# The head and the four preparation stages of a four-layer attention and mixture-of-experts kernel: load order, shared norms, prepared probabilities, a split subtraction

## The reference, cut to what matters

```python
def _prob(x):
    x = jnp.tanh(x) * 0.499 + 0.5
    return jnp.clip(x / (jnp.sum(x, axis=-1, keepdims=True) + EPS), EPS)
q_prob = _prob(q)                 # q = _layernorm(x)
k_prob = _prob(k)                 # k = v = ctx
log_ratio = jnp.log(q_prob) - jnp.log(k_prob)
sid = jnp.einsum('bnd,bmd->bnm', q_prob - k_prob, log_ratio)
attn = jax.nn.softmax(-sid / D ** 0.5, axis=-1)
attn_feat = jnp.einsum('bnm,bmd->bnd', attn, v)
f_diff = (v - attn_feat) @ W_diff.T + b_diff + q
h = _layernorm(f_diff, ln_g, ln_b)
out = gelu(h @ W1.T + b1) @ W2.T + b2 + f_diff     # then a layernorm
```

## Time and profile before

| what | us |
|---|---|
| median of 3 runs (lowest, highest) | 1151.25 (1150.07, 1156.2) |
| span of the profiled execution | 1143.9 |
| TensorE busy | 982.2 (86%) |
| VectorE busy | 742.5 (65%) |
| ScalarE busy | 478.9 (42%) |
| GpSimd busy | 280.5 (25%) |

### The profile page before, as it was taken

The page is one execution under the profiler, slowest core; times in us unless marked ns, Lnnn a source line. Parts: engine busy times, 40 slices in busy tenths (PEclk is TensorE's granted clock), DMA queues, the critical chain, the costliest instruction groups (busy, mean ns, idle before and its releaser), DMA issues.

```text
span 1143.9 us, 20648 instructions
## 1 busy us (share of the span) xinstructions
PE 982.2 (86%) x6905; PEld 591.4 (52%) x6905; DVE 742.5 (65%) x1952; ACT 478.9 (42%) x1055; POOL 280.5 (25%) x242
## 2 busy tenths in 40 slices
PE   7878789878898799999998876898899898987893
PEld 3555455546465488888885442333333333335662
DVE  3484677684878766666663476578777857545665
ACT  3443725342433344444442320446666657532331
POOL 0333524523320233444331001100010011112551
PEclk8999989998998899999999997669999988677997
DMA  8442020003535411111115486233163041231225
GB/s 289 150 129 110 2 74 1 19 1 93 142 98 166 146 49 53 49 53 48 48 40 164 96 152 126 54 42 53 43 112 75 2 131 61 87 126 37 79 76 176
DMA packets 69506, 98.64 MB, mean 86 GB/s; under 512 B 6528, under 2 KB 56960, under 8 KB 66976
## 3 DMA queue, kind: packets, MB, share of 16 engines
q1 hardware_dynamic: 60000, 63.75, 20.3%
q0 software_dynamic: 9408, 33.56, 11.0%
HBM read 70.10 MB, written 27.13 MB: 85 GB/s over the span
## 4 chain that ended last, share of the span: by engine, by line
PE 50%; DVE 28%; ACT 7%; DMA 7%; issue 4%; POOL 2%; SPq 1%; DVEq 0%; ACTq 0%; POOLq 0%
PE pb L1004 11%; PE pb L1021 7%; DVE MX L1943 5%; PE pb L1109 4%; PE pb L1022 3%; PE pb L769 3%; PE pb L1133 2%; PE pb L1087 2%; PE pb L848 2%; PE pb L838 2%; PE pb L792 2%; DMA xr<-rows,gi 2%; PE pb L1057 2%; ACT EX L1423 2%; DVE TQ L1552 1%
## 5 line engine op out<-in xcount | busy, mean ns | idle before, releaser
L1366 ACT ACTIVATE m<-pb,b1m 128x128 f32<-128x128 f32 x404 | 115.5, 369 | 172.0 <-PE pb L1004 169.8
L1423 ACT ACTIVATE EX<-pb 128x512 f32<-128x512 f32 x256 | 137.1, 599 | 115.7 <-PE pb L1133 114.9
L1943 DVE TENSOR_REDUCE MX<-pb 128x1 f32<-128x512 f32 x256 | 158.4, 683 | 41.0 <-PE pb L1087 40.8
L1004 PE MATMUL pb<-xt,w1h 128*128 128x128 f16 x1616 | 157.2, 221 | 3.8 <-issue 3.0
L1021 PE MATMUL pb<-w,mh 128*128 x404 | 149.4, 379 | 5.6 <-DVE ml L1854 5.2
L763 PE MATMUL pb<-identh 128*128 128x512 f16 x558 | 139.9, 408 | 15.5 <-DVE UZ L1588 8.8
L1004 PEld LDWEIGHTS pb<-xt,w1h 128*128 x1616 | 120.4, 99 | 42.0 <-issue 6.0
L1004 PE MATMUL pb<-xt,w1l 128*128 128x128 f16 x808 | 112.5, 220 | 0.0
L1022 PE MATMUL pb<-w,ml 128*128 x404 | 110.1, 273 | 0.0
L2155 POOL DMA_INDIRECT outs<-ob,di x62 | 61.3, 989 | 174.2 <-DVE ob L1869 174.2
L763 PEld LDWEIGHTS pb<-identh 128*128 128x128 f16 x558 | 55.9, 103 | 88.8 <-issue 21.4
(11 more groups left out here) (319 smaller groups left out, 1602.9 us busy)
## 6 DMA issues: line engine op xcount, KB each, us to landing
SR<-in_w1m SPq DMA_DIRECT2D x20, 512.0 KB, 5.6
SR<-in_w2m SPq DMA_DIRECT2D x14, 512.0 KB, 4.5
GB<-outs SPq DMA_DIRECT2D x12, 512.0 KB, 6.8
KS<-kd SPq DMA_DIRECT2D x48, 128.0 KB, 5.6
SRW<-in_w2m SPq DMA_DIRECT2D x10, 512.0 KB, 5.1
QS<-qd POOLq DMA_DIRECT2D x18, 256.0 KB, 10.1
kd<-KHL POOLq DMA_DIRECT2D x8, 512.0 KB, 5.7
vd<-VAB POOLq DMA_DIRECT2D x4, 1024.0 KB, 4.9
```

The costliest lines, as they stand in the source:

```text
L1004: ins = pe.matmul(k.ap[:, h4 * TOK:(h4 + 1) * TOK], wt[:, bass.ds(regs[j], 128)], M.xt[j % 2][:, xc, :], start=i == 0, stop=i == 5)
L1366: ins = act.activation(M.m32[x % 2][:, h4, :], k.ap[:, h4 * TOK:(h4 + 1) * TOK], M.func, bias=M.b1[:, bass.ds(reg + 4 * g + h4, 1)], scale ...
L1423: act.activation(EX[m % len(EX)][:, i, :], k.ap, ACT.Exp, scale=0.25).then_inc(k.out, 1)
L1943: v.tensor_reduce(mx[:, t, 2 * s + j:2 * s + j + 1], k.ap, AX.X, ALU.max).then_inc(k.out, 1)
```

## The change

The loads of x and of the context come first, `pp` has a semaphore of its own, and the bias rows come after the first transposed context. Batch 0's norm is taken alone; the sums of batches 1 to 3 are taken in steps 8 to 10 of `pre(0)` and their scalars together in step 11. ScalarE takes tanh straight from x, with the norm as scale and shift. VectorE scales the context's probabilities into a buffer `kp` (the tile XB) in step 5, and the q side is scaled and subtracted in one instruction per tile in step 7, once q's logarithms are out. GpSimd's subtraction of the logarithms is cut into two halves of the columns, and TensorE's transposes wait for each.

```diff
         LNZ = Zone(nc, SZ.start + 16 * K, 3 * K)
-        lnx, lnq, lno = ([stats(LNZ, f"{k}{i}", 4) for i in range(2)] for k in "xqo")
+        lnq, lno = ([stats(LNZ, f"{k}{i}", 4) for i in range(2)] for k in "qo")
+        lnx = [stats(LNZ, "x0", 4), stats(LNZ, "x1", 4 * (NB - 1))]
+        shx = [of[2] for of in lnx]
...
             def start():                                  # SyncE
+                load("x0", X[:, 0:4, :], xv[0])
+                load("c", CT[:, :, :], cv[0])
                 load("ident", ident[:, :], a["ident"])
-                load("x0", X[:, 0:4, :], xv[0])
+                load("pp", pp[:, :], a["pp"])
                 load("wc", Wqkv[:, 1:3, :, :], a["Wqkv"][:, 1:3])
+
+            def start_biases():
                 load("wa", WdT[:, :, :], a["WdT"])
-                load("wp", pp[:, :], a["pp"])
...
             def pre(b):                                   # SyncE
                 if b:
                     w.wait_ge(sem("tanh"), b)
-                load("c", CT[:, :, :], cv[b])
+                    load("c", CT[:, :, :], cv[b])
+                else:
+                    start_biases()
                 yield from pause(16)
...
                 for c in range(2):                        # TensorE
-                    w.wait_ge(sem("lgr"), b + 1)
+                    w.wait_ge(sem("lgr"), 2 * b + c + 1)
...
             def pre(b):                                   # ScalarE
-                yield from pause(2)
+                nt, sh, at = lnx[b > 0][3], shx[b > 0], 4 * (b - 1) if b else 0
+                yield from pause(2 if b else 1)
...
-                w.wait_ge(sem("q"), b + 1)
-                for t in range(4):
-                    ins = act.activation(TQ[:, t, :], Q[b % 3][:, t, :], ACT.Tanh, accum_out=sums[i][:, t:t + 1])
+                w.wait_ge(sem("sx"), 2 if b else 1)
+                for t in range(4):
+                    ins = act.activation(TQ[:, t, :], X[:, 4 * b + t, :], ACT.Tanh, scale=nt[:, at + t:at + t + 1], bias=sh[:, at + t:at + t + 1],
+                                         accum_out=sums[i][:, t:t + 1])
                 ins.then_inc(sem("tanh"), 1)
                 yield from pause(4)
                 w.wait_ge(sem("r"), b + 1)
-                w.wait_ge(sem("lgr"), b)
-                for src, dst, o in ((TQ, LQ, 0), (TC, LC, 4)):
+                w.wait_ge(sem("lgr"), 2 * b)
+                for src, dst, o, done in ((TQ, LQ, 0, "lnq"), (TC, LC, 4, "ln")):
...
-                ins.then_inc(sem("ln"), 1)
-                yield from pause(6)
+                    ins.then_inc(sem(done), 1)
+                yield from pause(6 if b else 7)
...
+            def x_scalars(n, of, sh):                     # VectorE
+                sc = ln_scalars(n, of)
+                v.scalar_tensor_tensor(out=sh[:, :], in0=of[1][:, :, 0], scalar=-1.0, in1=of[3][:, 0:n], op0=ALU.mult, op1=ALU.mult).then_inc(*c.up("sx"))
+                return sc
...
             def start():
...
-                w.wait_ge(sem("d_wp"), 8 * 16)
...
             def pre(b):                                   # VectorE
-                i, q = b % 2, Q[b % 3]
-                w.wait_ge(sem(f"d_x{b}"), 16)
-                sc = ln_stats([X[:, 4 * b + t, :] for t in range(4)], lnx[i])
-                for t in range(4):
-                    ins = v.tensor_scalar(q[:, t, :], X[:, 4 * b + t, :], *sc[t], ALU.subtract, ALU.mult)
+                i, q, r, kp = b % 2, Q[b % 3], rr8[b % 2], XB
+                if b == 0:
+                    w.wait_ge(sem("d_x0"), 16)
+                    ln_sums([X[:, t, :] for t in range(4)], lnx[0])
+                    xs[0] = x_scalars(4, lnx[0], shx[0])
+                for t in range(4):
+                    ins = v.tensor_scalar(q[:, t, :], X[:, 4 * b + t, :], *xs[b][t], ALU.subtract, ALU.mult)
                 ins.then_inc(*c.up("q"))
                 yield from pause(5)
...
-                r_ready = c.last
-                yield from pause(4)
-                w.wait_ge(*r_ready)
-                w.wait_ge(sem("ln"), b + 1)
-                for src, o in ((TQ, 0), (TC, 4)):
-                    for t in range(4):
-                        ins = v.tensor_scalar(src[:, t, :], src[:, t, :], r[:, 8 + o + t:9 + o + t], r[:, 16 + o + t:17 + o + t], ALU.mult, ALU.add)
+                w.wait_ge(*c.last)
+                v.tensor_tensor(r[:, 0:4], r[:, 20:24], r[:, 16:20], ALU.subtract).then_inc(*c.up("v"))
+                w.wait_ge(*c.last)
+                for t in range(4):
+                    ins = v.tensor_scalar(kp[:, t, :], TC[:, t, :], r[:, 12 + t:13 + t], r[:, t:t + 1], ALU.mult, ALU.add)
                 ins.then_inc(*c.up("v"))
-                w.wait_ge(*c.last)
-                v.tensor_tensor(TQ[:, :, :], TQ[:, :, :], TC[:, :, :], ALU.subtract).then_inc(*c.up("dif"))
-                yield from pause(3)
+                kp_done = c.last
+                yield from pause(2)
+                w.wait_ge(*kp_done)
+                w.wait_ge(sem("lnq"), b + 1)
+                for t in range(4):
+                    ins = v.scalar_tensor_tensor(out=TQ[:, t, :], in0=TQ[:, t, :], scalar=r[:, 8 + t:9 + t], in1=kp[:, t, :], op0=ALU.mult, op1=ALU.subtract)
+                ins.then_inc(*c.up("dif"))
+                yield
+                for b2 in range(1, NB):
+                    if b == 0:
+                        w.wait_ge(sem(f"d_x{b2}"), 16)
+                        ln_sums([X[:, 4 * b2 + t, :] for t in range(4)], lnx[1], 4 * (b2 - 1))
+                    yield
+                if b == 0:
+                    sc = x_scalars(4 * (NB - 1), lnx[1], shx[1])
+                    xs.update({b2: sc[4 * (b2 - 1):4 * b2] for b2 in range(1, NB)})
+                yield
...
             def pre(b):                                   # GpSimd
                 yield from pause(9)
                 w.wait_ge(sem("ln"), b + 1)
-                pool.tensor_tensor(LQ[:, :, :], LQ[:, :, :], LC[:, :, :], ALU.subtract).then_inc(sem("lgr"), 1)
+                for c in range(2):
+                    cols = slice(c * 128, (c + 1) * 128)
+                    pool.tensor_tensor(LQ[:, :, cols], LQ[:, :, cols], LC[:, :, cols], ALU.subtract).then_inc(sem("lgr"), 1)
```

More of the change, by code:

```diff
@@ L1502, in ln_stats, with ln_scalars @@
                         w.wait_ge(*ready[i])
-                    ins = v.bn_stats(st[:, i, :], t)
+                    ins = v.bn_stats(of[0][:, at + i, :], t)
                 ins.then_inc(*c.up("v"))
+            def ln_scalars(n, of):
+                st, mv, ve, tmp = of
                 w.wait_ge(*c.last)
-                for i in range(len(tiles)):
+                for i in range(n):
                     ins = v.bn_aggr(mv[:, i, :], st[:, i, :])
@@ L1622, in kv @@
             def kv(b):
+                w.wait_ge(sem("d_pp"), 16)
                 for cc in range(2):
```

20 lines of the change are left out of this document (12 added, 8 removed).

## The result

| | before | changed |
|---|---|---|
| median of 20 runs each (lowest, highest), us | 1150.54 (1140.13, 1157.96) | 1137.62 (1131.3, 1151.25) |
| profiled execution: time, span, us | not listed, 1143.9 | 1143.88, 1142.1 |
| TensorE, VectorE, ScalarE, GpSimd busy, us | 982.2, 742.5, 478.9, 280.5 | 982.3, 735.6, 482.2, 281.5 |
| TQ transposes of batch 0, 1, 2, 3 | 38.07, 90.28, 153.49, 217.99 | 31.28, 82.58, 144.35, 206.11 |
| first matmul of the first expert (L1011 now) | 385.84 | 372.54 |

The medians differ by 12.9 us. The ratio over the runs of both kernels that are in the fast state is 0.9924 with a 95% interval of 0.9898 to 0.9949, which is 8.7 us (5.9 to 11.7) of 1150.54. So the sign is clear, and the size is known to a few microseconds only. The forecast was 1135.7, the sum of the parts 15.6.

What follows compares the result with a forecast made beforehand. No engine fills the span; time is lost where TensorE and VectorE wait for each other. Terms 3.5 + 2.2 + 3.0 + 4.0 + 2.9 = 15.6 us take span 1143.9 to 1128.3, plus 7.35 forecasts 1135.7; range 1127 to 1145.

Steps and rivals of the forecast that it cites:

- Head: Start to batch 0's TQ transposes: earlier loads and projection gain 4.4 us, less 0.9 for lower clock behind a wait: −3.5.
- Work put beside the head: Sums of batches 1 to 3 and scalars on VectorE, steps 8 to 11: covered, 0; up to 2 if not.
- rest(0): TensorE's 2.21 us wait at 61.38, while VectorE takes batch 1's norm before evicting, should all go: −2.2 us.
- Batch 1's preparation: The 3.59 idle before the transposes and the half clock behind it go, UZ's eviction comes later: −3.0 us.
- Batch 2's: Batch 2's preparation: gains of 7.9 us, less 3.9 for scalings waiting on two GpSimd operations in step 5: −4.0.
- Batch 3's: Batch 3's preparation: 1.56 from the norm gone, 1 from UZ's eviction, 0.35 from other evictions: −2.9 us.
- The distance of 7.35: Us by which the median of runs lay above the profiled span, added to span 1128.3 to forecast 1135.7.
- The four signs against it: Projection past 16.5; round 0's UZ wait above 5; round 1's GT above 8; offset at 220 shrinking over 3 before experts.
- the clean case: Rival: batch 2's step 5 scalings meet no GpSimd work and the clock stays up: 22.5 us gained, 1128.7; chance 0.22.
- does not do what it says: Rival: first loads no faster, `ident` lands past 12, the head loses 2: −10, 1141; chance 0.08.
- slower: Rival: each step 5 scaling waits for a GpSimd operation, UZ's eviction 7 us late in batches 1–3: +9, 1160.5; chance 0.03.
- Absorbed later: Rival: later loads, or new waits in rounds 0 to 2, eat all but head and `rest(0)`: −5.7, 1145.5; chance 0.12.

Runs made afterwards that it cites:

- f1: The changed kernel once more, with nothing altered: median of 6 runs 1137.04 us, ratio to the kernel before 0.9905.
- e6: Changed kernel with ScalarE's logarithms of batch 0 in step 6 instead of 5, behind the third value tile's eviction: 1139.12 us.
- f4: Changed kernel with the edits of f3 and e6 together: median of 6 runs 1132.7 us, ratio to the kernel before 0.9867.
- e3: Changed kernel with the eight scalings and the subtraction of the kernel before in step 9, nothing added in step 5: 1124.95 us.
- e4: Changed kernel with the small subtraction and the context's four scalings moved from step 5 to step 6, behind UZ's eviction: 1125.24 us.
- f3: Changed kernel with the context's scalings in step 6 and the two-input instructions in step 8, behind VAB's eviction: median of 8 runs 1135.19 us.
- e8: Changed kernel with eighteen clears of a tile on VectorE ahead of the cast of ident, starting the fill 16.3 us later: 1146.44 us.
- e1: Kernel before with the load order of the change and nothing else: 1140.44 us.

## Why the prediction was right, and where it was not

The time, 1137.62, lies 1.9 above the forecast and inside the range. The gain was forecast too large: 15.6 us, where the medians give 12.9, the ratio 8.7 (5.9 to 11.7) and f1's medians 10.1. The range around the time was wide enough for that. By the parts, each against the lead at its end:

**Head, −3.5: measured −6.8, or −2.7 to −4.2 in the other runs where the clock fell.** The mechanism held: fill first, projection at full clock, tanh of the context and most of the norm under the fill, the wait for the value tile behind the logarithms. Mis-sized were three things. `ident` landed 4.28 after its issue, so that the cast came at 6.07 and not near 6.6. The fill took 6.66 us, taken as 8.19; over the runs it took 6.66 to 8.25. And ScalarE's logarithms ended at 23.96, not 26.3, because the scalars were out at 11.85 and the first projection began at 12.86, forecast 15.1; the four tanhs of x took 0.59 each, where those of the context took 0.40, and this cost nothing. The 0.9 for a lower clock behind the wait was a mean of two cases. Of ten profiles with this wait of 3.50 to 3.52, TensorE went on at 2.4 GHz in three (heads of 24.9 to 25.0) and at 1.2 in seven (27.4 to 28.9, a part of the difference being a longer fill). The fill sorts them: it took 6.66 to 6.74 us in the three and 6.83 to 8.20 in the seven. That is what the traces show, and no run tests it. The windows view of the first profile, then of f1, behind the same wait:

```profile
24.10:28.00 3.90, 3.72 (x17) 2.58 (x18) 3.04 (x9) 0.39 (x2) 2.43 (x2) 1.00 1.08 386
```

```profile
25.00:31.50 6.50, 6.12 (x16) 3.48 (x17) 3.25 (x10) 0.60 (x3) 2.49 (x2) 0.55 0.97 348
```

So the usual gain is 2.7 to 4.2, with the forecast inside, and the first profile was the lucky case. Part of the cost was the change's own: with batch 0's logarithms a step later the wait is 1.77 and 1.78, and 2.4 GHz followed it both times (e6, f4).

**Work put beside the head, 0: right.** The scalars for twelve tiles end at 33.68, the next key tiles are evicted behind them with no wait of TensorE.

**`rest(0)`, −2.2: right, −2.4,** and −2.3 to −2.4 in every variant with the norms in the head.

**Batch 1's preparation, −3.0: measured −0.2.** This is the step that failed most. UZ's wait rose to 3.97 (forecast 4.2) with 3.4 us at 1.2 GHz behind it, as assumed. But the growth of the wait did not bring these: in e3, e4 and f3 the same fill took 5.75 behind waits of 2.35 to 2.38, in the kernel before 4.06 behind 2.57. With that lower clock the prediction's own sum gave 2.0, and taking 3.0 was 1.0 too much. What the sum had no term for was step 7: I let it "end long before the transposes" and asked only when TQ would be ready, not what stands behind it on VectorE. The four instructions took 5.48 us beside GpSimd's low halves and the new halves of LQ, and held VAB's eviction, for which TensorE waits 1.98; that is most of the rest. The chance was named: that the two-input form stalls if step 7 meets low halves, "when it is 2 us longer and still early". It was 3.8 longer (5.48 − 1.67). The rule of the Trainium skill (SBUF — State Buffer, Who interferes with whom), that such an instruction of VectorE is held while GpSimd reads SBUF, agrees with these rows: 5.48 and 4.35 beside GpSimd, 1.67 and 1.66 without.

**Batch 2's, −4.0: measured −3.2** (9.4 to 12.6), 1.3 of it by the norm gone from `rest(1)`, forecast 1. Both halves were as forecast: the scalings waited for two or three GpSimd operations (5.09 us), UZ came late, GT's wait grew to 6.20 (near 6), the fills behind it took 5.67 at half clock, and in return the transposes and the product ran without a wait for VectorE at full clock, 7.13 us for the product. The gains named add up to 7.9, the better end of the range says 8.2; nothing hangs on it.

**Batch 3's, −2.9: measured +0.7 at the transposes, −0.7 at the first expert** (12.6 to 11.9 and 13.3). The norm's part came, 1.8 by round 2's transposes of UZ (forecast 1.56). But I had UZ's own transposes cover the new scalings and UZ's eviction gain 1. `r` was held as before (2.10 at 175.47), the subtraction of four columns took 1.00 and the scalings 1.38 more, and TensorE waited 3.31 for the eviction, with 6.8 us at 0.50 from 179.70 (3.4 us in f1). e4 and f3, with the scalings behind the eviction, have 0.85 there and 1.0 throughout: that difference is what showed the cause. The step that failed is the cover: UZ's own transposes ended before the scalings did.

**Sum.** −15.6 against −13.3 in the first profile (11.7 in f1). The first profile's surplus in the head, 3.3, hid that batches 1 and 3 gave 0.9 us together instead of 5.9: that the sum came near was in part luck. The step from span to time held a second error. The distance of 7.35 compared a median with one profile's span; every run in which both are known has 1.8, and the runs of before scatter over 18 us. It did no harm, since the same distance stood on both sides.

**What was named as showing right or wrong.** Transposes at 31.28, not 33.6; no wait in `rest(0)` and none for TQ, right; full clock from batch 2's product on, right for the product and wrong behind it (0.50 from 179.70); batch 3's transposes 13 to 18 earlier, wrong at 11.9. The four signs against it did not appear: projection at 12.86, UZ's wait under 5, GT's under 8, and from 11.8 at 237 us the lead did not shrink by the experts, it was 13.3. Of the rivals, *the clean case* is out by the 5.09 us of batch 2's scalings, *does not do what it says* by the landings, *slower* by the medians. *Absorbed later* is out by e8 as far as loads and later waits go; its other half, new waits that eat what batches 1 to 3 bring, came true for batches 1 and 3 and not for batch 2.

Not settled: why the same wait of 3.5 us is followed by 1.2 GHz in some executions and not in others, and what draws the stretches at 1.2 GHz in the tail. No run here changes either on purpose. Nor is the length of the first fill tried, though the projection now waits for it.

## What to carry to other kernels

When a step moves on a shared in-order engine, price what stands behind it there, at its stalled length, before asking whether its own result is in time: the new scaling form saved instructions, and the stretch was 1.3 to 3.5 us longer than with the old form until the scalings stood behind UZ's eviction and the two-input instructions behind VAB's. Even a small instruction of VectorE on tiles in SBUF can last as long as a GpSimd operation beside it, so it belongs behind whatever feeds TensorE. Where the granted clock scatters a tail by 18 us, compare variants by the time at which one and the same matmul starts and by several runs, and never by one span.

## What the runs showed of the hardware

- A VectorE instruction of 8 columns (0.16 us alone) lasted 2.38 beside a GpSimd addition of 2.36 that started in the same moment (65.58 and 65.57). Not every instruction is held: in the kernel before UZ's eviction, which reads TensorE's output, took 1.52 at 129.56 beside the addition at 129.51, as it does elsewhere.
- Tanh with a scale and a shift for each partition took 0.59 us for 128x256, without them 0.40.
- The same wait of 3.5 us was followed by full clock in three profiles and by half in seven, in one and the same program too (the changed kernel's first profile and f1). From the end of the fill to the transposes this is worth 1.4 to 3.1 us. A shorter wait can be followed by half clock as well: behind 2.21 the product took 5.43 in e1 and 3.75 in the kernel before.
- With one and the same load order, `ident` third in the queue, the fill started between 6.27 and 7.56 in twelve profiles.
